# Six transformer layers: the layer loop written out, with another table of empty instructions on TensorE

## The reference, cut to what matters

```python
for i in range(DEPTH):
    x = attn_layer(shift_tokens(x), Wqkv[i], q_scale[i], k_scale[i], Wo[i]) + x
    x = ffn_layer(shift_tokens(x), ln_g[i], ln_b[i], W1[i], b1[i], W2[i], b2[i]) + x

def attn_layer(x, Wqkv, qs, ksc, Wo):
    q, k, v = 16 heads of 64, from x @ Wqkv          # 128 x 3072
    q, k = l2norm(q) * qs, l2norm(k) * ksc           # then a scaled rotary turn
    out = local_attention(q, k, v)                   # windows of 32 with a look back of 32
    return out @ Wo
def ffn_layer(x, g, bln, W1, b1, W2, b2):
    a, gate = jnp.split(layernorm(x) @ W1 + b1, 2, -1)
    return a * jax.nn.gelu(gate, approximate=False) @ W2 + b2
```

## Time and profile before

| what | value |
|---|---|
| median of 3 runs | 3418.55 us (3417.37 to 3420.17) |
| the profiled execution | 3418.27 us |
| its span, first to last instruction | 3416.5 us |
| mean granted PE clock | 0.973 of full speed |
| PE busy | 3188.8 us (93%) |
| DVE busy | 2812.1 us (82%) |
| ACT busy | 2597.2 us (76%) |
| POOL busy | 2626.1 us (77%) |
| chain that ended last | PE 70%, ACT 15%, issue 8%, DVE 5%, POOL 2% |

### The profile page before, as it was taken

How to read it: one execution, slowest core, us unless ns; L and a number is a source line. 1 busy time by engine, 2 the same in 40 slices (tenths; PEclk the granted TensorE clock), 3 DMA queues, 4 the chain that set the end, 5 groups by cost and what they waited for, 6 DMA issues and landing times.

```text
span 3416.5 us, 133004 instructions
## 1 busy us (share of the span) xinstructions
PE 3188.8 (93%) x52802; PEld 2706.0 (79%) x52802; DVE 2812.1 (82%) x3743; ACT 2597.2 (76%) x3707; POOL 2626.1 (77%) x2593
## 2 busy tenths in 40 slices
PE   7978999989999989999989999989999999999996
PEld 4647888878788878888878888878888878888885
DVE  7967888888788888888888888888878888888882
ACT  6746778877787878778777877878778777878874
POOL 6648888878877878878878878877878887888871
PEclk9979999999999999999999999999999999999997
DMA  1001111111111111111101111111111111111111
GB/s 63 2 10 36 58 39 33 38 28 44 52 43 38 35 31 41 43 56 35 40 27 46 36 58 39 33 33 39 40 59 33 38 35 38 37 40 33 38 35 29
DMA packets 57827, 130.82 MB, mean 38 GB/s; under 512 B 10992, under 2 KB 33136, under 8 KB 56432
## 3 DMA queue, kind: packets, MB, share of 16 engines
q1 hardware_dynamic: 57200, 121.94, 12.2%
HBM read 19.17 MB, written 2.10 MB: 6 GB/s over the span
## 4 chain that ended last, share of the span: by engine, by line
PE 70%; ACT 15%; issue 8%; DVE 5%; POOL 2%; ACTq 0%; DMA 0%; POOLq 0%; DVEq 0%; SPq 0%
PE pair L211 56%; PE pair L214 13%; ACT qT L855 10%; ACT sq L845 3%; DVE ts L977 1%; ACT ss L850 1%; DVE ss L981 1%; DVE mx L998 1%; DVE qk L973 0%; DVE pair L994 0%; DVE tab L955 0%; POOL qk L1080 0%; DVE tab L956 0%; DVE Sx L1002 0%; ACT sq L837 0%
## 5 line engine op out<-in xcount | busy, mean ns | idle before, releaser
L1101 POOL TENSOR_TENSOR qk<-qk,ts 128x1024 f32<-128x1024 f32 x384 | 912.4, 2385 | 228.8 <-DVE ts L977 213.5
L973 DVE TENSOR_TENSOR qk<-pair,tab 128x1024 f32<-128x1024 f32 x384 | 468.2, 1219 | 365.6 <-ACT sq L837 362.8
L1080 POOL TENSOR_TENSOR qk<-qk,rn 128x1024 f32<-128x1024 f32 x384 | 733.1, 1930 | 28.6 <-issue 13.5
L211 PE MATMUL pair<-wq_h,xs_h 128*128 128x512 f32 x1154 | 512.3, 444 | 31.6 <-issue 14.8
L832 ACT ACTIVATE Sx<-Sx 128x1024 f32<-128x1024 f32 x192 | 203.4, 1060 | 395.4 <-DVE Sx L1002 395.4
L214 PE MATMUL pair<-small,qk 128*128 128x128 f32 x3104 | 420.5, 279 | 75.4 <-ACT qT L855 54.5
L1112 POOL TENSOR_TENSOR Sx<-Sx,rden 128x1024 f32<-128x1024 f32 x192 | 365.3, 1902 | 157.2 <-DVE rden L1032 157.2
L211 PE MATMUL pair<-wq_h,xs_l 128*128 128x512 f32 x1152 | 469.7, 408 | 0.4
L211 PE MATMUL pair<-wq_l,xs_h 128*128 128x512 f32 x1152 | 468.4, 407 | 0.0
L977 DVE TENSOR_TENSOR ts<-pair,tab 128x1024 f32<-128x1024 f32 x384 | 466.0, 1214 | 0.0
L981 DVE TENSOR_REDUCE ss<-sq 128x16 f32<-128x1024 f32 x384 | 463.9, 1208 | 0.0
(11 more groups left out here) (126 smaller groups left out, 6678.6 us busy)
## 6 DMA issues: line engine op xcount, KB each, us to landing
VB<-VA SPq DMA_DIRECT2D x192, 384.0 KB, 3.5
VB<-VA SPq DMA_DIRECT2D x96, 128.0 KB, 3.5
wq_raw<-wqkv SPq DMA_DIRECT2D x6, 1536.0 KB, 7.2
xf<-xT SPq DMA_DIRECT2D x96, 64.0 KB, 1.9
xf<-xT SPq DMA_DIRECT2D x96, 63.8 KB, 2.0
wo_sb<-wo SPq DMA_DIRECT2D x6, 512.0 KB, 3.6
X<-x_in SPq DMA_DIRECT2D x4, 512.0 KB, 7.6
out<-X SPq DMA_DIRECT2D x8, 256.0 KB, 2.3
```

The costliest lines, as they stand in the source:

```text
L211: return T_.matmul(out, lhsT, rhs, start=start, stop=stop, **k)
L973: V_.tensor_tensor(h3(qk[:, now, kind, :], DH), h3(source[:, :], DH), rep(tab[:, 2 * kind, b, :], HEADS, DH), ALU.mult)
L1080: G_.tensor_tensor(x, x, bc(rn[:, then, kind * HEADS:(kind + 1) * HEADS], HEADS, DH), ALU.mult).then_inc(S["scaled"], 1)
L1101: G_.tensor_tensor(qk[:, now, kind, :], qk[:, now, kind, :], ts[:, kind, :], ALU.add).then_inc(S["added"], 1)
```

## The change

The loop over the first five layers is replaced by a Python loop, so that all six layers are written out for every engine; the last one is still built with `last` set. The waits in the first five layers compare with constants. The table `FILL` has other numbers: 56 and 19 for most pairs of steps, where it had 45 or 46 and 21 or 22. `FILL_AHEAD` is 21 where it was 6. `fill` itself is as it was.

```diff
@@ -616,16 +616,13 @@
             pl = Place(e, 0)
             for t in range(DRAIN):
                 step(e, pl.at(t))
-            with e.Fori(0, DEPTH - 1) as i:
-                pl = Place(e, i)
+            for turn in range(DEPTH):
+                pl = Place(e, turn, turn == DEPTH - 1)
                 for t in range(DRAIN, DRAIN + NBLOCKS):
                     step(e, pl.at(t))
-            pl = Place(e, DEPTH - 1, True)
-            for t in range(DRAIN, DRAIN + NBLOCKS):
-                step(e, pl.at(t))
-
-        FILL = (43, 21, 46, 21, 44, 22, 47, 21, 46, 22, 48, 20, 39, 21, 45, 21, 45, 22, 46, 21, 45, 22, 46, 21, 45, 22, 46, 21, 45, 22, 46, 21)
-        FILL_AHEAD = 6
+
+        FILL = (53, 20, 56, 19, 56, 19, 56, 19, 56, 19, 56, 19, 56, 19, 56, 19, 56, 19, 56, 19, 56, 19, 56, 19, 56, 19, 56, 19, 56, 19, 56, 19)
+        FILL_AHEAD = 21
```

## The result

| what | before | after |
|---|---|---|
| median | 3417.96 us (3416.63 to 3420.17) | 3467.28 us (3462.67 to 3470.97) |
| profiled execution, its span | 3418.27, 3416.5 us | 3470.97, 3469.2 us |

What follows compares the result with a forecast made beforehand. PE, busy 93% of the span, was taken as the bound, so time changes only where it stands or is fed slowly. 3418.3 - 22 (jumps) - 20 (long even steps) + 91 (table) = 3467 us, range 3436 to 3491.

Steps and rivals of the forecast that it cites:

- The jumps: Four places where the loop jumps back: the two steps around each lose 5.0 to 6.1 us; unrolling gives -22 us.
- The long even steps: Every second even step in the loop, 16.51 us at an instruction piece's edge, falls to 16.0: -20 us together.
- the new edges hurt nowhere: Edges move into V, score and feed-forward matmuls and behind odd steps' second transposes, where they should cost nothing.
- C: Rival: edge falls into second transposes of every second odd step, 45 steps by 0.3 to 0.77 us, 3481 to 3502; chance 0.09.
- The table: Even steps go from mostly 45 or 46 empty instructions to 56 behind the projection matmuls: 17.0 us each, +91 us in all.
- v: Three empty instructions behind each of v's six projection matmuls in even steps delay the feed-forward's first load: +0.7 us a step.
- q and k: More empty instructions behind q's and k's projection matmuls in even steps delay k's transposes: +0.3 us a step.
- The signs named ahead: In even steps, k's transposes at 4.6 us instead of 4.33, first feed-forward load at some 10.8 instead of 9.73.
- The sentence on register instructions: Removing the register instructions with which the loop computes its waits is worth nothing: written-out even step 16.00, loop's short one 15.98.
- A: Rival: the table costs nothing, the step is bound elsewhere and PE's stream catches up, 3376 us; chance 0.09.
- B: Rival: only v pays, q and k hide under ACT's copy; even step 16.7, 3441 us; chance 0.11.
- D: Rival: the long steps keep their half microsecond at another even position, 3487 us; chance 0.09.

Runs made afterwards that it cites:

- the run with 33 ahead: Changed kernel with FILL_AHEAD 33 in place of 21, every edge 12 instructions earlier in its step: 3492.54 us, ratio 1.0219 to the kernel before.
- the one with 66: Kernel before, loop and table untouched, with FILL_AHEAD 66 in place of 6, every edge 60 instructions earlier: 3407.84 us, ratio 0.9967.
- 45 and 30: Changed kernel with 45 empty instructions in even and 30 in odd steps in place of 56 and 19: 3366.66 us, ratio 0.9854 to the kernel before.
- the run with four: Changed kernel with four empty instructions, not three, behind v's six matmuls in even steps, 13 in odd steps, FILL_AHEAD 15: 3551.05 us.
- v as before: Changed kernel with two empty instructions, not three, behind v's six matmuls in even steps, those six moved to odd steps: 3399.05 us.
- 45 and 30 and 13 ahead: Changed kernel with 45 and 30 empty instructions in even and odd steps and FILL_AHEAD 13 in place of 21: 3367.22 us, ratio 0.9853.

## Why the prediction was right, point by point

**The jumps, -22.** Held: -22.3, and no step of 19 us is left. The kernel that keeps the loop keeps them whatever the table (19.59 us). The run written out with the old table, in which only the loop is gone, shows the same: -22.2. That a jump fetches pieces again is what the packets say (457 where the instructions make 449.2); how the 5 to 6 us of a jump divide between that fetch and the rest, no run tells.

**The long even steps, -20.** Held in size: -19.6. That an edge between pieces of PE's instructions is at work rests on the run with 33 ahead (a shift by 12 places lengthens one kind of step in four by 0.45 us, from 15.21 to 15.66, and no other) and on the one with 66 (a shift by 60 shortens the long kind by 0.3). So the edge is shown for 0.3 of the 0.5 us; what the other 0.2 us were is open, though the whole change did away with them too. My statement that the new edges hurt nowhere was a little too good. 12 of the 45 odd steps of the kind that carries an edge are 15.35 to 15.45 instead of 15.11, with a stall in their second transposes:

```profile
2745.43 0.64 PEld L214 LDWEIGHTS pair<-small,qk 128*128 128x128 f32 x6 [0.31 <-issue]
2746.42 0.20 PEld L214 LDWEIGHTS pair<-small,qk 128*128 128x128 f32 x2 [0.35 <-issue]
```

That is C in small, +4 us. The margin was thin, as the prediction said: 12 instructions of shift bring C in full. The Trainium skill, "Runtime: NRT & Kernel Launch", Instruction fetch mechanics, calls the crossing of such a boundary mostly hidden. The runs agree for most crossings: a pair of steps holds four or five edges, and most steps of the 45 and 30 kernel are 15.11 and 16.00 us long. They do not agree at a bad place, where a step is 0.55 us longer in the mean (15.66 for 15.11), and 3.0 us at the worst seen (18.13 for 15.11, in the run with the old table), the slow clock included.

**The table, +91.** The largest term, and the mechanism is shown. Even step 17.06 against the 17.0 forecast; v 0.71 against 0.7; q and k 0.38 against 0.3 (against the 45 and 30 kernel the medians of the first transposes come 0.09 us later and those of q 0.38, so q has 0.09 and k 0.29 of it, where I had counted 0.15 and 0.15); an empty instruction 0.155 us each in the run with four, against 0.151 read off before. The signs named ahead were the transposes behind k at 4.6 us (4.63 in the step shown, 4.71 in the median) and the first feed-forward load at 10.8 (10.89 and 10.94). The steps at the layer changes and at the start cost +4.6 against before and +6.0 against 45 and 30, where I had estimated 6. The term is a few us too small: against the kernel with the same count spread 45 and 30 it is 3467.28 - 3366.66 = 101, of which 90 in the even steps.

**The sentence on register instructions** ("worth nothing") is true of the kernel before and not in general. Written out with 45 in the even step, the usual even step is 16.01 us (the run with the old table), no shorter than in the loop; with 56 the even steps of the loop are 0.44 us longer. The prediction was safe from this only because both parts of the change came together. The run with the table alone was expected too low for this reason.

**What offset what.** Written out with a table that holds the edges and lies under cover, the kernel is at 3367, 9 us below the 3376 to which the prediction came before its table term. That term was about as much too small. The profiled spans show the 9 us outside the terms that I had: -2.4 before the first step, -4.4 behind the last, -1.4 in the layer changes and the first twelve. None of the three is isolated, and the stretch before the first step is 233 to 239 us in the kernels here without a cause that I can name. That forecast and median agree to 0.3 us is therefore luck: the four executions of the changed kernel lie between 3463 and 3471.

**The rivals.** A (the table costs nothing) falls by the runs with v as before and with four, and by 45 and 30: near its 3376, at 3367, stands the kernel whose empty instructions lie elsewhere. B (only v pays) falls too: q and k cost 0.36 to 0.38 us. D (the long steps stay) falls, since all 85 even steps lie within 0.4 us of each other. C holds in small here, and in full once the edge is shifted.

## What to carry to other kernels

An instruction that does nothing is free only under a stream that has time to spare: count its price (here 0.15 us) against the matmul that covers it, in each step by itself, and put the filler where that balance is positive (11 more in the odd step cost nothing, 11 more in the even one 1.06 us). If a step's length differs for the same work at a fixed period, look for the edge of the instruction pieces, and shift it with a few instructions at the program's start, which is the cheapest experiment there is. Unrolling and refitting such a table are separate changes with their own signs (-0.7% for the first alone, +2.9% for this table against the 45 and 30 one), so time them apart.

## What the runs showed of the hardware

- A stall at an edge can be followed by a slower clock: 1.40 us of standing, then a granted clock of 0.54 for 3.7 us. The clock fell in six ordinary steps of the runs that are written out (three without empty instructions, two with the old table, one with 45 and 30 and 13 ahead), each time behind 1.0 to 1.5 us of standing among the matmuls on V. These six are 18.1 to 18.7 us long, and no other ordinary step of these three runs is over 17.4. The length of the stall alone does not decide it: 1.43 us (t = 179 without empty instructions) and the 1.14 us of the run with 33 ahead left the clock at 1.00. What does, no run here tells. The Trainium skill, "TensorE: Matmul & The Clock Gate", What's actually happening, tells of a clock at half rate after the engine has idled; the row agrees as to the halving.
- Fewer instructions are not faster by themselves: without any empty instruction the kernel is 46 us slower than with 75 a pair under cover. The edges that wander are the part of it that the trace shows; that the stream also runs through its pieces faster is a second possible part, which no run separates.
- An empty instruction takes 0.151 us of PE's instruction stream, from the trace and from six more of them (0.93 us). A register instruction for a wait takes about 0.11 us of it by the trace (0.10 to 0.11 between the quartiles). Both cost time only where the stream has none to spare.
- A jump of the loop goes with one or two more packets of instructions for PE (457 for 449.2 pieces with four jumps, and 458 for 452.4), and its two steps together are 5.0 to 6.1 us longer.
